# A three-part decoder layer on one core: heads-first projections, rotation by transferred halves, plain fp32 self scores

## The chip, the cores and the metric

The kernel runs on one core of a Trainium2 chip. The core has TensorE (matmuls and transposes, written PE in the rows), VectorE (DVE), ScalarE (ACT), GpSimd (POOL) and SyncE (SP), whose queue issues the transfers here. Each engine works through its own list of instructions in order and waits on semaphores. Times are microseconds (us) of one execution on the device; lower is better.

## What is computed

32 sequences of 256 tokens with 256 features go through three blocks, each added to its input and normalized. Only the first one is touched by the change: 16 query heads and 4 key and value heads of 64 features, a rotation by position, a bias linear in the distance, softmax, and the output weights. Cut to this:

```python
q = (x @ Wq).reshape(b, l, H, HD).transpose(0, 2, 1, 3)
k = (x @ Wk).reshape(b, l, KV, HD).transpose(0, 2, 1, 3)
v = (x @ Wv).reshape(b, l, KV, HD).transpose(0, 2, 1, 3)
...
q = q * cos + _rotate_half(q) * sin      # halves (x1, x2) -> (-x2, x1)
k = k * cos + _rotate_half(k) * sin
attn = jnp.einsum('bhqd,bhkd->bhqk', q, k) / math.sqrt(HD)
attn = attn + slopes[None, :, None, None] * rel[None, None, :, :]
out = jnp.einsum('bhqk,bhkd->bhqd', jax.nn.softmax(attn, axis=-1), v)
...
x = _layernorm(x + self_attention(x))
x = _layernorm(x + window_attention(x, ctx, tokens))
x = _layernorm(x + quantized_gated_ffn(x))
```

The second block is attention of windows of 64 positions to the context, the third a feed-forward part with quantized activations and three-valued weights.

## The kernel before

One batch (a sequence) is cut into named steps, and every engine has a written list of steps: `HEAD`, then `BODY` repeated with the batch number moved on by one, then `TAIL`. The repeated order runs for 27 of the 32 batches. An entry such as `(2, 'QX')` means step `QX` of the batch two behind the newest one, so three or four batches are in work at once. There is no scheduler: what stands in the list is the order of the engine, and an engine that waits holds up all that stands behind it in its list. The waits themselves are written by step kind (`at`, `freed`), so a step waits for its data and for the PSUM bank it writes, until the step that read the bank's last content has emptied it (`EMPTIED`).

The steps that the text names, in the order of the data:

- `X` splits the loaded `xT` into `x_hi` (ScalarE) and `x_lo` (GpSimd). `K`, `V` and four `Q` steps (token tile 0 or 1, column half 1 or 2) project it on TensorE by `project` (L660), each as three rounded fp32 products (high with high, low with high, high with low), tokens on partitions. ScalarE copies `Q` to `qtok` (L1353), VectorE multiplies the exchanged halves by the sines into `by_sin` (L1027), GpSimd multiplies by the cosines and adds (L1457, L1460). For `K` VectorE makes both products (L1015, L1017) and GpSimd adds (L1451).
- `kT` and `qT 0` to `qT 3` transpose the rotated tiles, so that head features lie on partitions (L644, `ktok` and `qtok`). ScalarE writes the rounded high part from PSUM, VectorE the low part (L1032, L1037).
- `S 0` to `S 7` are the self scores of two heads each (L760), again three rounded products, two heads at once on the two 64-row halves of the array. VectorE adds the distance bias and takes the row maximum (L1046), ScalarE takes the exponential (L1372), VectorE the reciprocal of the sum (`R`, L1053) and GpSimd divides (`R`, L1464).
- `T 0` to `T 15` transpose the probabilities, ScalarE copies them (L1379). `O 0` to `O 3` multiply by the values (L779), plain fp32. `W 0`, `W 1` are the output weights (L790).
- `YS`, `X1`: statistics and normalization of the sum. `NX`: its transposes; `QX`: the cross query projection, `QXT`: its transposes. `KV 0`, `KV 1`: cross keys and values from the context (L814), `KXT`: their transposes (L644, `kx_tok`), after which VectorE adds a bias (L1138) and SP fills the padded tile `kx` by eight transfers (`fill_kx`, L623). `SX 0` to `SX 3` are the cross scores, plain fp32 (L832 and L839), on banks 5 and 6; `TX`, `OX`, `BX`, `NO`, `PO` lead on to the second block's result.
- `XQ`, `G`, `U`, `HS`, `HT`, `D`, `ZS`, `out`: the third block in bf16 (L891, L901, L653, L914).

Bank 7 serves one after another `NX`, `XQ`, `QX`, `KXT`, `QXT`, `HT`, `OX`, `D`, `BX`, `NO`, `PO` and `KV`. Some fill matmuls without use (L718) stand in `HEAD` and `TAIL` only.

Of the kernel before, what the change touches and what calls it, by code (L numbers as in the profile page):

```python
# [73 lines left out]

BODY = {
    "sp": [
        (2, 'load_cell'), (3, 'load_vs'), (2, 'load_ctxT'), (3, 'fill_kx'), (2, 'load_xtok'), (2, 'load_ctx'),
        (0, 'load_xT'), (4, 'store'),
    ],
# [44 lines left out]
    "sp": [  # L124
        (0, 'first', 0), (0, 'first', 1), (0, 'first', 2), (0, 'load_xT'), (0, 'tables', 0), (0, 'loads', 0),
        (0, 'loads', 1), (0, 'load_cell'), (0, 'load_xtok'), (0, 'tables', 1), (0, 'loads', 2), (0, 'load_ctx'),
        (1, 'load_xT'), (0, 'load_ctxT'), (2, 'load_xT'), (1, 'load_ctxT'), (0, 'kx_clear'), (0, 'fill_kx'),
        (1, 'load_ctx'), (1, 'load_xtok'), (0, 'load_vs'), (1, 'load_cell'), (2, 'load_cell'), (3, 'load_xT'),
        (2, 'load_xtok'), (2, 'load_ctxT'), (1, 'load_vs'), (2, 'load_ctx'), (1, 'fill_kx'), (0, 'store'), (4, 'load_xT'),
    ],  # L130
# [1485 lines left out]
```

## Time and profile before

| what | us |
|---|---|
| median of 3 runs | 2222.89 |
| lowest and highest | 2222.48, 2224.62 |
| the profiled execution | 2226.64 |
| its span in the trace | 2224.7 |
| TensorE, VectorE, ScalarE, GpSimd busy | 2139.7, 1906.7, 1699.2, 1420.7 |

The profiled execution is 3.75 above the median, and 1.9 of it lie outside the span. A row of a timeline has the start, the length of the record, the engine, the line of the kernel, the instruction with the tile that it writes and those that it reads, and a count of instructions merged into the row; a bracket at its end is idle time ahead of it. Matmul records overlap, since the next one starts before the last one has drained: how long a step holds TensorE is read from its start to the start of the next row. A row such as `x1` where two were issued lacks a record, and the step began a little earlier.

### The profile page before, as it was taken

How to read it: one execution, taken by the hardware profiler on the slowest of the kernel's cores; microseconds unless marked ns; L12 is line 12 of the kernel's file. 1: busy time of each engine (PE TensorE's matmuls, PEld its weight loads, DVE VectorE, ACT ScalarE, POOL GpSimd, SP SyncE). 2: the span in 40 equal slices, each digit the busy share in tenths (PEclk: the TensorE clock that was granted, in tenths of full speed). 3: DMA queues.
4: the chain of work that ended last, by engine and by line, in shares of the span. 5: the costliest groups of instructions: out<-in, count | busy, mean ns of one | idle time of the engine just before them, and what ended most of it. 6: DMA issues, size and time to landing. Idle time of an engine off the chain costs nothing. (4 is left out here: it accounts for less than half of the span.)

```text
span 2224.7 us, 58431 instructions
## 1 busy us (share of the span) xinstructions
PE 2139.7 (96%) x19659; PEld 1665.7 (75%) x19722; DVE 1906.7 (86%) x7884; ACT 1699.2 (76%) x4746; POOL 1420.7 (64%) x1670
## 2 busy tenths in 40 slices
PE   7899999999999999999999999999999999999986
PEld 6677777777777777777777777777777777777764
DVE  5778888888988889988888898888988888889876
ACT  4687778887778887777888777888777788877752
POOL 2566666666766666776666676666677666667531
PEclk9999999999999999999999999999999999999999
DMA  4010101101110110110110111011011111011100
GB/s 165 11 35 25 37 25 35 27 25 37 37 36 24 28 37 26 37 37 25 35 28 25 37 37 34 26 28 37 26 37 37 25 35 28 25 37 37 27 21 11
DMA packets 85399, 74.68 MB, mean 34 GB/s; under 512 B 18544, under 2 KB 79344, under 8 KB 85104
## 3 DMA queue, kind: packets, MB, share of 16 engines
q1 hardware_dynamic: 85104, 70.93, 11.8%
q8 instruction: 163, 2.67, 0.5%
q14 instruction: 132, 1.08, 0.2%
HBM read 45.72 MB, written 8.39 MB: 24 GB/s over the span
## 5 line engine op out<-in xcount | busy, mean ns | idle before, releaser
L1464 POOL TENSOR_TENSOR prob<-prob,precs 128x512 f32<-128x512 f32 x512 | 528.5, 1040 | 551.3 <-DVE precs L1053 548.0
L1372 ACT ACTIVATE prob<-prob,nmax 128x256 f32<-128x256 f32 x1024 | 508.6, 504 | 46.0 <-DVE nmax L1046 46.0
L1046 DVE CUSTOM_DVE_ANT_0 prob<-bank,alibi 128x256 f32<-128x256 f32 x1024 | 371.5, 419 | 23.3 <-PE bank L760 23.2
L1379 ACT COPY pT<-bank 128x512 f32<-128x512 f32 x512 | 302.8, 591 | 57.0 <-PE bank L644 55.8
L644 PE MATMUL bank<-ident,prob 128*128 128x128 f32 x2048 | 316.0, 277 | 3.5 <-ACT pT L1379 3.0
L1396 ACT ACTIVATE px<-px,nmx 128x128 f32<-128x128 f32 x1024 | 313.7, 398 | 6.2 <-DVE nmx L1158 6.2
L644 PEld LDWEIGHTS bank<-ident,prob 128*128 128x128 f32 x2048 | 231.1, 141 | 55.5 <-issue 39.2
L779 PE MATMUL bank<-pT,v_sb 128*64 128x256 f32 x2048 | 250.4, 387 | 4.0 <-DVE qq_lo L1037 3.6
L1158 DVE CUSTOM_DVE_ANT_0 px<-bank,mask 128x128 f32<-128x128 f32 x1024 | 226.4, 287 | 3.7 <-issue 1.7
L779 PEld LDWEIGHTS bank<-pT,v_sb 128*64 128x64 f32 x2048 | 137.2, 137 | 101.2 <-issue 39.9
L1460 POOL TENSOR_TENSOR qtok<-qtok,by_sin 128x512 f32<-128x512 f32 x128 | 164.7, 1287 | 56.0 <-DVE by_sin L1027 46.1
L1372 ACT ACTIVATION_READ_ACCUMULATOR prob<-prob,nmax 128x1 f32 x1024 | 198.2, 194 | 0.0
L660 PE MATMUL bank<-w_hi,x_hi 128*128 128x256 f32 (+1 forms) x512 | 190.5, 372 | 4.0 <-POOL x_lo L1444 1.5
L1417 ACT ACTIVATE hh<-bank,ax 128x512 f32<-128x512 f32 x128 | 88.2, 689 | 133.2 <-PE bank L891 133.1
L1457 POOL TENSOR_TENSOR qtok<-qtok,rope 128x512 f32<-128x512 f32 x128 | 164.9, 1288 | 33.4 <-ACT qtok L1353 33.4
L660 PE MATMUL bank<-w_lo,x_hi 128*128 128x256 f32 (+1 forms) x512 | 173.2, 338 | 0.0
L660 PE MATMUL bank<-w_hi,x_lo 128*128 128x256 f32 (+1 forms) x512 | 172.8, 337 | 0.0
L760 PE MATMUL bank<-kk_hi,qq_hi 64*128 64x256 f32 x1024 | 170.6, 330 | 1.5 <-DVE kk_lo L1032 1.0
L644 PE MATMUL bank<-ident,px 128*128 128x128 f32 x1032 | 160.2, 278 | 7.3 <-ACT px L1396 2.9
L1403 ACT COPY pTx<-bank 128x512 f32<-128x512 f32 x252 | 146.5, 581 | 12.6 <-PE bank L644 12.5
L790 PE MATMUL bank<-wo_hi,oT_hi 128*128 128x256 f32 x512 | 146.2, 286 | 0.0
L760 PE MATMUL bank<-kk_hi,qq_lo 64*128 64x256 f32 x1024 | 144.2, 278 | 0.0
(223 smaller groups left out, 5950.0 us busy)
## 6 DMA issues: line engine op xcount, KB each, us to landing
raw<-in_xT SPq DMA_DIRECT2D x32, 256.0 KB, 3.0
xtok<-in_x SPq DMA_DIRECT2D x32, 256.0 KB, 2.9
kx_tok<-in_ctx SPq DMA_DIRECT2D x32, 256.0 KB, 3.0
raw<-in_ctxT SPq DMA_DIRECT2D x32, 256.0 KB, 3.0
kx<-k_sin SPq DMA_DIRECT2D x256, 32.0 KB, 2.0
vs<-vx SPq DMA_DIRECT2D x64, 128.0 KB, 2.3
out_y<-x SPq DMA_DIRECT2D x31, 256.0 KB, 3.2
cellk<-in_cell SPq DMA_DIRECT2D x32, 64.0 KB, 3.8
```

What stands on the lines that cost most here:

```text
L644: last = nc.tensor.transpose(bank[:, n * P:(n + 1) * P], src, ident[:])
L660: last = mm(to, xs[:, k, t * P:(t + 1) * P], ws[:, k, cols], start=i == 0, stop=i == KT * 3 - 1)
L760: last = mm(psum[SCORES[c]][:, q * L:(q + 1) * L], qs[half, u % 2, m, q * P:(q + 1) * P], ks[half, p // 4, :], start=i == 0, stop=i == 2)
L779: last = mm(psum[bank][c * HD:(c + 1) * HD, m * L:(m + 1) * L], v_sb[:, k, g * HD:(g + 1) * HD], pT[:, m, c, k, :], start=k == 0, stop=k = ...
L1046: v.tensor_tensor_reduce(out=prob[:, (2 * p + q) % SLOTS, c, :], in0=psum[SCORES[c]][:, q * L:(q + 1) * L], in1=alibi[:, p % 2, :], scale= ...
L1158: v.tensor_tensor_reduce(out=px[:, s % 2, i, :], in0=psum[xscores(b)[r]][:, h * P:(h + 1) * P], in1=mask[:, s % 2, :], scale=-1.0, scalar= ...
L1372: nc.scalar.activation(prob[:, (2 * p + q) % SLOTS, c, :], prob[:, (2 * p + q) % SLOTS, c, :], ACT.Exp, bias=nmax[:, i:i + 1], scale=-1.0, ...
L1379: nc.scalar.copy(pT[:, p % 2, :, :, q * P:(q + 1) * P].rearrange("p c k n -> p (c k) n"), bank[:].rearrange("p (c n) -> p c n", c=4)).then ...
L1396: ins = nc.scalar.activation(px[:, s % 2, i, :], px[:, s % 2, i, :], ACT.Exp, bias=nmx[:, 8 * s + i:8 * s + i + 1], scale=-1.0)
L1457: g.tensor_tensor(heads, heads, rope[:, 0, t:t + 1, :].to_broadcast([P, 8, HD]), ALU.mult).then_inc(sem["q_cos"], 1)
L1460: g.tensor_tensor(qtok[:, t, :], qtok[:, t, :], by_sin[:], ALU.add).then_inc(sem["rot_sum"], 1)
L1464: g.tensor_tensor(prob[:, n % SLOTS, :, :], prob[:, n % SLOTS, :, :], precs[:, 2 * n:2 * n + 2].unsqueeze(2).to_broadcast([P, 2, L]), ALU. ...
```

## The change

- `K` and the `Q` steps become five units `proj 0` to `proj 4` (unit 1 is the keys, 0, 2, 3 and 4 are the query groups 0 to 3). The weights are now the stationary operand and the tokens run through, so a unit has twelve 256-wide products, and the result has head features on partitions. `kT` and `qT` are gone.
- ScalarE writes a unit, with its scale, from the bank into `flat`. SP exchanges the halves of 32 partitions by four transfers of 64 KB into `swap`. VectorE multiplies the bank by the cosines into `turn`. GpSimd multiplies `swap` by the sines and adds `turn`, into `kk` (two buffers) or `qq` (one per group). `flat`, `swap` and `turn` have two buffers each.
- The self scores are four plain fp32 products in place of twelve rounded ones.
- The rotation table lies with features on partitions. `ZS` on GpSimd has one more wait, for `out` of the batch before. The GpSimd scratch space for transfers is made smaller.
- All step lists are written anew. Steps of the second and third block have moved too, and so have the fills in `HEAD` and `TAIL`.

```diff
+                    elif kind == "swap":
+                        n, = args
+                        i = (UNITS * b + n) % 2
+                        sp.wait_ge(*at("raw_ready", b, n))
+                        sp.wait_ge(*at("rot_sum", b, n - 2))
+                        for r in range(4):
+                            sp.dma_start(swap[r * 32:(r + 1) * 32, i, :, :], flat[(r ^ 1) * 32:(r ^ 1) * 32 + 32, i, :, :])\
+                                .then_inc(swapped[i], 16)
...
+                    elif kind == "proj":
+                        pe.wait_ge(*at("x_lo", b))
+                        pe.wait_ge(*freed(sem, bank, steps, place))
+                        parts = ((x_hi, w_hi), (x_lo, w_hi), (x_hi, w_lo))
+                        for m in range(2):
+                            first = (m if n == 1 else 4 + 2 * GROUP[n] + m) * P
+                            for i in range(KT * 3):
+                                k, (xs, ws) = i // 3, parts[i % 3]
+                                last = mm(psum[bank][:, m * L:(m + 1) * L], ws[:, k, first:first + P], xs[:, k, :], start=i == 0, stop=i == KT * 3 - 1)
...
-                        parts = ((qq_hi, kk_hi), (qq_lo, kk_hi), (qq_hi, kk_lo))
                         for q in range(2):
-                            for i, (qs, ks) in enumerate(parts):
-                                for c in range(2):
-                                    half = slice(c * HD, (c + 1) * HD)
-                                    last = mm(psum[SCORES[c]][:, q * L:(q + 1) * L], qs[half, u % 2, m, q * P:(q + 1) * P],
-                                              ks[half, p // 4, :], start=i == 0, stop=i == 2)
+                            for c in range(2):
+                                half = slice(c * HD, (c + 1) * HD)
+                                last = mm(psum[SCORES[c]][:, q * L:(q + 1) * L], qq[half, u, m, q * P:(q + 1) * P],
+                                          kk[half, b % 2, p // 4, :], start=True, stop=True)
...
+                    elif kind == "turn":
+                        dve.wait_ge(*at("raw_ready", b, n))
+                        dve.wait_ge(*at("rot_sum", b, n - 2))
+                        v.scalar_tensor_tensor(out=turn[:, i, :, :], in0=psum[home(b, "proj", n)][:].rearrange("p (m n) -> p m n", m=2),
+                                               scalar=1.0 if n == 1 else 0.125 / FACTOR[GROUP[n]],
+                                               in1=rope[:, 0:1, :].to_broadcast([P, 2, L]), op0=ALU.mult, op1=ALU.mult).then_inc(sem["rot_cos"], 1)
...
+                    elif kind == "flat":
+                        act.wait_ge(*at("proj_mm", b, n))
+                        act.wait_ge(*unit_swapped(b, n - 2))
+                        nc.scalar.activation(flat[:, i, :, :], psum[home(b, "proj", n)][:].rearrange("p (m n) -> p m n", m=2), ACT.Copy,
+                                             scale=1.0 if n == 1 else 0.125 / FACTOR[GROUP[n]]).then_inc(sem["raw_ready"], 1)
...
+                    elif kind == "turn":
+                        pool.wait_ge(*unit_swapped(b, n))
+                        g.tensor_tensor(swap[:, i, :, :], swap[:, i, :, :], rope[:, 1:2, :].to_broadcast([P, 2, L]), ALU.mult).then_inc(sem["rot_sin"], 1)
+                        pool.wait_ge(*at("rot_sin", b, n))
+                        pool.wait_ge(*at("rot_cos", b, n))
+                        pool.wait_ge(*at("S_mm", b - 1, 2 * GROUP[n] + 1 if n != 1 else -1))
+                        g.tensor_tensor(kk[:, b % 2, :, :] if n == 1 else qq[:, GROUP[n], :, :], turn[:, i, :, :], swap[:, i, :, :], ALU.add)\
+                            .then_inc(sem["rot_sum"], 1)
```

The order of VectorE in the repeated part, around the bias sum of `KXT` (the row that writes `k_sin` with 512 elements). Before, the sum stands behind `U 1` and the low part of `qT 3`, and `HS 0` follows:

```order
L1251 SCALAR_TENSOR_TENSOR hh<-hh,bank 128x512
L1255 TENSOR_TENSOR hh<-hh,bank 128x512
L1037 SCALAR_TENSOR_TENSOR qq_lo<-bank,q_scale,qq_hi 128x512
L1138 TENSOR_TENSOR k_sin<-bank,turned_bias 128x512
L1259 TENSOR_REDUCE hs<-hh 128x1
```

In the changed kernel (its own line numbers), the last of the four score instructions of `S 5` and their maximum, then `turn 1`, then the sum:

```order
L1031 ISA prob,nmax<-bank,alibi 128x256
L1031 ISA nmax 128x1
L1021 SCALAR_TENSOR_TENSOR turn<-bank,rope 128x512
L1123 TENSOR_TENSOR k_sin<-bank,turned_bias 128x512
L1236 SCALAR_TENSOR_TENSOR hh<-hh,bank 128x512
L1240 TENSOR_TENSOR hh<-hh,bank 128x512
L1244 TENSOR_REDUCE hs<-hh 128x1
```

So `S 5` has moved from behind the sum to ahead of it. The order of TensorE at the end of the feed-forward part, in bank 7. Before, with `wd` the down weights (`D 0`, `D 1`) and `hh` the transposes of `HT 1`:

```order
L914 MATMUL bank7<-wd16,hqT 128x256 x8
L644 MATMUL bank3<-ident,px 128x128 x4
L644 MATMUL bank2<-ident,prob 128x128 x4
L653 MATMUL bank7<-ident16,hh 128x128 x8
```

In the changed kernel the same two steps, with `D 1` behind them:

```order
L921 MATMUL bank7<-wd16,hqT 128x256 x8
L672 MATMUL bank7<-ident16,hh 128x128 x8
L663 MATMUL bank2<-ident,prob 128x128 x4
L663 MATMUL bank3<-ident,px 128x128 x4
L921 MATMUL bank7<-wd16,hqT 128x256 x8
```

`HT 1` now follows `D 0` with nothing between them. SP's order in the repeated part of the changed kernel, from `load_vs` on:

```order
L648 DMA vs<-vx 64x512
L649 DMA vs<-vx 64x512
L627 DMA raw<-in_ctxT 128x2x256
L621 DMA xtok<-in_x 128x2x256
L642 DMA kx<-k_sin 16x2x256 x8
L616 DMA swap<-flat 32x512 x4
L630 DMA cellq<-in_cell 128x2x1
```

Before it was

```order
L629 DMA vs<-vx 64x512
L630 DMA vs<-vx 64x512
L608 DMA raw<-in_ctxT 128x2x256
L623 DMA kx<-k_sin 16x2x256 x8
L602 DMA xtok<-in_x 128x2x256
```

so `load_xtok` has moved ahead of the fills, and a swap follows them.

## Rows read from the trace of the kernel before

**Rows 1.** The page, section 1: busy us, share of the span, instructions.

```profile
PE 2139.7 (96%) x19659; PEld 1665.7 (75%) x19722; DVE 1906.7 (86%) x7884; ACT 1699.2 (76%) x4746; POOL 1420.7 (64%) x1670
```

**Rows 2.** TensorE's timeline (start, length, engine, line, instruction, count): `V` of two batches.

```profile
1034.13 0.29 PE L660 MATMUL bank<-w_hi,x_hi 128*128 128x256 f32 x1
...
1035.58 0.60 PE L644 MATMUL bank<-ident,qtok 128*128 128x128 f32 x4
...
1099.93 0.28 PE L660 MATMUL bank<-w_hi,x_hi 128*128 128x256 f32 x1
```

**Rows 3.** TensorE's timeline: `kT`, `D 0` and the transposes behind them.

```profile
1076.93 0.60 PE L644 MATMUL bank<-ident,ktok 128*128 128x128 f32 x4
1077.67 1.03 PE L914 MATMUL bank<-wd,hqT 128*128 128x256 bf16 x8
1078.54 0.60 PE L644 MATMUL bank<-ident,px 128*128 128x128 f32 x4
1078.97 0.60 PE L644 MATMUL bank<-ident,prob 128*128 128x128 f32 x4
```

**Rows 4.** TensorE's timeline: `S 5`, `O 1`; then `SX 0` and `W 0`.

```profile
1052.77 0.39 PE L760 MATMUL bank<-kk_hi,qq_hi 64*128 64x256 f32 x2
...
1053.68 1.95 PE L779 MATMUL bank<-pT,v_sb 128*64 128x256 f32 x16
1055.56 0.65 PE L644 MATMUL bank<-ident,prob 128*128 128x128 f32 x4
...
1060.18 1.13 PE L832 MATMUL bank<-kx,qx 64*128 64x512 f32 x4
1061.24 0.39 PE L790 MATMUL bank<-wo_hi,oT_hi 128*128 128x256 f32 x1
```

**Rows 5.** TensorE's timeline: a `Q` step, a `T` step, a score step.

```profile
1057.27 0.48 PE L660 MATMUL bank<-w_hi,x_hi 128*128 128x512 f32 x1
...
1058.74 0.60 PE L644 MATMUL bank<-ident,prob 128*128 128x128 f32 x4
1059.27 0.39 PE L760 MATMUL bank<-kk_hi,qq_hi 64*128 64x256 f32 x2
```

**Rows 6.** TensorE's timeline: steps with waits; the last has it in brackets.

```profile
1040.92 0.65 PE L644 MATMUL bank<-ident,prob 128*128 128x128 f32 x4
1041.68 0.63 PE L644 MATMUL bank<-ident,xtok 128*128 128x128 f32 x4
1042.06 0.36 PE L660 MATMUL bank<-w_hi,x_hi 128*128 128x256 f32 x1
...
1043.80 0.38 PE L653 MATMUL bank<-ident,q_sin 128*128 128x128 bf16 x4
...
1068.88 1.13 PE L832 MATMUL bank<-kx,qx 64*128 64x512 f32 x4 [0.28 <-DVE nmx L1158]
```

**Rows 7.** VectorE's timeline: `qT 3`, sum of `KXT`; `S 5` and what follows it.

```profile
1051.74 0.75 DVE L1037 SCALAR_TENSOR_TENSOR qq_lo<-bank,q_scale,qq_hi 128x512 fp32r<-128x512 f32 x1
1052.40 0.68 DVE L1138 TENSOR_TENSOR k_sin<-bank,turned_bias 128x512 f32<-128x512 f32 x1
...
1056.74 0.42 DVE L1046 CUSTOM_DVE_ANT_0 prob<-bank,alibi 128x256 f32<-128x256 f32 x1
...
1058.12 0.68 DVE L1251 SCALAR_TENSOR_TENSOR hh<-hh,bank 128x512 f32<-128x512 f32 x1
```

**Rows 8.** SP's timeline of the fills; the page's DMA row (KB, us).

```profile
1053.11 5.13 SPq L623 DMA_DIRECT2D kx<-k_sin  x8
...
kx<-k_sin SPq DMA_DIRECT2D x256, 32.0 KB, 2.0
```

**Rows 9.** GpSimd's timeline: `YS` begins, `K`'s sum, `R 8` with `R 9`.

```profile
1045.06 0.23 POOL L1471 TENSOR_SCALAR y_var<-y_mv 128x2 f32<-128x2 f32 x1
...
1049.59 1.31 POOL L1451 TENSOR_TENSOR ktok<-ktok,by_sin 128x512 f32<-128x512 f32 x1
1050.85 2.05 POOL L1464 TENSOR_TENSOR prob<-prob,precs 128x512 f32<-128x512 f32 x2
```

More of the change, by code:

```diff
@@ L72 @@
 RAW = 8
+UNITS = 5
+GROUP = {0: 0, 2: 1, 3: 2, 4: 3}
 BODY = {
[L76 to L79, printed above, removed]
     "pe": [
[10 rows of a table removed]
[10 rows of a table added]
     ],
     "dve": [
[10 rows of a table removed]
[9 rows of a table added]
     ],
     "act": [
[8 rows of a table removed]
[8 rows of a table added]
     ],
     "pool": [
[4 rows of a table removed]
[5 rows of a table added]
+    ],
+    "sp": [
+        (3, 'load_vs'), (2, 'load_ctxT'), (2, 'load_xtok'), (3, 'fill_kx'), (1, 'swap', 1), (2, 'load_cell'),
+        (2, 'load_ctx'), (1, 'swap', 2), (0, 'load_xT'), (1, 'swap', 3), (1, 'swap', 4), (4, 'store'), (0, 'swap', 0),
     ],
@@ L123 @@
 HEAD = {
[L124 to L130, printed above, removed]
@@ L166 @@
     ],
     "dve": [
-        (0, 'first', 0), (0, 'first', 1), (0, 'first', 2), (0, 'prep', 0), (0, 'tables', 0), (0, 'K'), (0, 'Q', 0, 1),
-        (0, 'prep', 1), (0, 'prep', 2), (0, 'prep', 3), (0, 'Q', 1, 1), (0, 'prep', 4), (0, 'tables', 1), (0, 'qT', 0),
[30 rows of a table removed]
+        (0, 'first', 0), (0, 'first', 1), (0, 'first', 2), (0, 'prep', 0), (0, 'tables', 0), (0, 'turn', 0),
+        (0, 'turn', 1), (0, 'prep', 1), (0, 'prep', 2), (0, 'prep', 3), (0, 'prep', 4), (0, 'tables', 1),
+        (0, 'wo_split'), (0, 'turn', 2), (0, 'S', 0), (0, 'R', 0), (0, 'R', 1), (0, 'S', 1), (0, 'R', 2),
@@ L200 @@
+        (0, 'turn', 3), (0, 'prep', 6), (0, 'S', 2), (0, 'R', 3), (0, 'prep', 7), (0, 'S', 3), (0, 'turn', 4),
[27 rows of a table added]
     ],
     "act": [
-        (0, 'first', 0), (0, 'first', 1), (0, 'first', 2), (0, 'X'), (0, 'tables', 0), (0, 'Q', 0, 1), (0, 'Q', 1, 1),
[28 rows of a table removed]
+        (0, 'first', 0), (0, 'first', 1), (0, 'first', 2), (0, 'X'), (0, 'flat', 0), (0, 'tables', 0), (0, 'flat', 1),
+        (0, 'flat', 2), (0, 'prep', 4), (0, 'wo_split'), (0, 'S', 0), (0, 'S', 1), (0, 'V'), (0, 'flat', 3),
[26 rows of a table added]
     ],
     "pool": [
[15 rows of a table removed]
+        (0, 'X'), (0, 'turn', 0), (0, 'turn', 1), (0, 'R', 0), (0, 'turn', 2), (0, 'R', 1), (0, 'turn', 3),
[13 rows of a table added]
@@ new lines @@
+        (3, 'turn', 4),
+    ],
+    "sp": [
+        (0, 'first', 0), (0, 'tables', 0), (0, 'load_xT'), (0, 'first', 1), (0, 'first', 2), (0, 'loads', 0),
+        (0, 'swap', 0), (0, 'load_ctx'), (0, 'loads', 1), (0, 'load_cell'), (1, 'load_xT'), (0, 'swap', 1),
+        (0, 'tables', 1), (0, 'loads', 2), (0, 'swap', 2), (0, 'swap', 3), (0, 'swap', 4), (0, 'load_ctxT'),
+        (0, 'load_xtok'), (1, 'swap', 0), (1, 'swap', 1), (1, 'swap', 2), (1, 'swap', 3), (1, 'load_cell'),
+        (1, 'swap', 4), (2, 'load_xT'), (2, 'swap', 0), (0, 'fill_kx'), (1, 'load_ctx'), (1, 'load_ctxT'),
+        (1, 'load_xtok'), (2, 'swap', 1), (0, 'load_vs'), (2, 'swap', 2), (3, 'load_xT'), (2, 'load_cell'),
+        (2, 'swap', 3), (2, 'swap', 4), (1, 'load_vs'), (3, 'swap', 0), (2, 'load_xtok'), (2, 'load_ctxT'),
+        (3, 'swap', 1), (1, 'fill_kx'), (3, 'swap', 2), (2, 'load_ctx'), (3, 'swap', 3), (4, 'load_xT'), (0, 'store'),
+        (3, 'swap', 4), (4, 'swap', 0),
@@ L251 @@
 TAIL = {
[L252 to L256 removed]
[22 rows of a table removed]
[19 rows of a table added]
+        (31, 'fill', 3, 8), (31, 'G', 3), (31, 'HT', 0), (31, 'fill', 5, 4), (31, 'fill', 3, 16), (31, 'fill', 5, 4),
+        (31, 'D', 0), (31, 'HT', 1), (31, 'D', 1), (31, 'fill', 3, 8),
     ],
     "dve": [
[18 rows of a table removed]
[16 rows of a table added]
     ],
     "act": [
[13 rows of a table removed]
[13 rows of a table added]
     ],
     "pool": [
[7 rows of a table removed]
[8 rows of a table added]
+    ],
+    "sp": [
+        (29, 'load_vs'), (30, 'load_xtok'), (30, 'load_ctxT'), (30, 'load_cell'), (29, 'fill_kx'), (30, 'load_ctx'),
+        (31, 'swap', 1), (31, 'swap', 2), (31, 'swap', 3), (31, 'load_ctxT'), (31, 'swap', 4), (28, 'store'),
+        (31, 'load_cell'), (30, 'load_vs'), (31, 'load_xtok'), (30, 'fill_kx'), (31, 'load_ctx'), (29, 'store'),
+        (31, 'fill_kx'), (31, 'load_vs'), (30, 'store'), (31, 'store'),
     ],
@@ L337 @@
 EMPTIED["prep", 5] = ("w_mean", 0)
-EMPTIED.update({("qT", u): ("q_ready", u) for u in range(4)})
+EMPTIED.update({("proj", n): ("rot_cos", n) for n in range(UNITS)})
 EMPTIED.update({("O", u): ("oT_ready", u) for u in range(4)})
@@ L417, in at, with unit_swapped @@
             return (sem[name], count) if count > 0 else (sem["begun"], 1)
+        swapped = [ctx.enter_context(nc.semaphore(f"swapped{i}")) for i in range(2)]
+        def unit_swapped(batch, n):
+            unit = UNITS * batch + n
+            return (swapped[unit % 2], 64 * (unit // 2 + 1)) if unit >= 0 else (sem["begun"], 1)
         def landed(name, batch):
@@ L464, in build @@
         v_sb = sb("v_sb", [P, TT, KV * HD])
-        by_sin = sb("by_sin", [P, 512])
-        ktok = sb("ktok", [P, TT, KV * HD])
-        qtok = sb("qtok", [P, TT, 8 * HD])
-        kk_hi = sb("kk_hi", [P, 2, L], F32R)
-        kk_lo = sb("kk_lo", [P, 2, L], F32R)
-        qq_hi = sb("qq_hi", [P, 2, 2, L], F32R)
-        qq_lo = sb("qq_lo", [P, 2, 2, L], F32R)
+        flat = sb("flat", [P, 2, 2, L])
+        swap = sb("swap", [P, 2, 2, L])
+        turn = sb("turn", [P, 2, 2, L])
+        kk = sb("kk", [P, 2, 2, L])
+        qq = sb("qq", [P, 4, 2, L])
         prob = sb("prob", [P, SLOTS, 2, L])
@@ L730, in run @@
                         last.then_inc(sem["V_mm"], 1)
-                    elif kind == "Q":
-                        t, c = args
-                        pe.wait_ge(*freed(sem, bank, steps, place))
-                        pe.wait_ge(*at("x_lo", b))
-                        project(2, t, psum[bank][:], slice(512 * c, 512 * c + 512)).then_inc(sem["proj_mm"], 1)
-                    elif kind == "kT":
-                        pe.wait_ge(*at("rot_sum", b, 0))
-                        pe.wait_ge(*freed(sem, bank, steps, place))
-                        transposes(psum[bank], [ktok[:, t, h * P:(h + 1) * P] for h in range(2) for t in range(TT)])\
-                            .then_inc(sem["kT_mm"], 1)
-                    elif kind == "qT":
-                        u, = args
-                        pe.wait_ge(*at("rot_sum", b, 2 if u < 2 else 4))
-                        pe.wait_ge(*freed(sem, bank, steps, place))
-                        transposes(psum[bank], [qtok[:, t, (2 * (u % 2) + m) * P:(2 * (u % 2) + m + 1) * P]
-                                                for m in range(2) for t in range(TT)]).then_inc(sem["qT_mm"], 1)
                     elif kind == "S":
@@ L1572, in constants @@
     cos, sin = rope_table(L, HD, 0)
-    rope = np.concatenate([by_tile(cos), by_tile(sin * np.where(np.arange(HD) < HD // 2, -1.0, 1.0))], axis=1)
+    turned = np.stack([cos, sin * np.where(np.arange(HD) < HD // 2, -1.0, 1.0)]).transpose(0, 2, 1)
+    rope = np.concatenate([turned, 2.0 * turned], axis=1).transpose(1, 0, 2).reshape(P, 2 * L)
     rel = (np.arange(L)[None, :] - np.arange(P)[:, None]).astype(np.float32)
     alibi = np.stack([np.float32(2.0 ** (-0.5 - m / 2)) * rel for m in range(2)], axis=1).reshape(P, -1)
-    q_scale = np.array([[0.125 / FACTOR[u] * 4.0 ** (p // HD) for u in range(4)] for p in range(P)])
     ropex = []
@@ L1586, in constants @@
     second = k > WIN + q % WIN
-    return dict(rope=f(rope), alibi=f(alibi), q_scale=f(q_scale), ropex=f(np.concatenate(ropex, axis=1)), pen=f(np.concatenate([first, second], axis=1)))
+    return dict(rope=f(rope), alibi=f(alibi), ropex=f(np.concatenate(ropex, axis=1)), pen=f(np.concatenate([first, second], axis=1)))
 def kernel(**inputs):
```

96 lines of the change are left out of this document (21 added, 75 removed), and 382 rows, old and new, of tables (BODY, HEAD, TAIL).

## The prediction

> **What bounds the kernel now.** I read the page's busy shares first, then TensorE's timeline over one batch, then what each engine waits for in that stretch. TensorE is busy for 96% of the span, VectorE for 86%, ScalarE for 76%, GpSimd for 64% [rows 1]. A busy share alone doesn't prove a bound, because a matmul's record is longer than the slot it takes: the reader should go by the distance from one start to the next. The value projection of one batch starts at 1034.13 and that of the next at 1099.93, so a batch takes 65.80 us [rows 2]. Walking through that batch, step start to step start, almost every step begins where the one before leaves off. The visible waits are few: 0.31 behind the key transposes [rows 3], and in [rows 6] 0.31 before the transposes of `NX` (0.76 where 0.45 is usual), 0.29 between `K` and `XQ` (1.74 where 1.45 is usual) and 0.28 before a cross score step. They sum to 1.19 us. So about 64.6 of the 65.8 us are matmul slots, and the kernel is bound by TensorE's slots. Work taken from the other engines counts only where TensorE waits for it.
>
> **Transposes removed.** Four `qT` steps and `kT` go, each four fp32 transposes. Neighbouring transposes of that shape stand 0.43 apart, and the step after a product in another form takes a little more [rows 3]; I take 0.44. Five of them in 32 batches: 5 x 0.44 x 32 = 70 us off. They lie on TensorE itself, so all of it counts.
>
> **Projections.** Before, a `Q` step of six 512-wide products takes 1.47, and there are four; `K` has twelve 256-wide ones, like `V`, whose twelve take 1.45 [rows 2, 5]. After, there are five units of twelve 256-wide products. 4 x 1.47 + 1.45 = 7.33 becomes 5 x 1.45 = 7.25, with the same number of columns. The doubled number of weight loads doesn't show in `V`. I add 0.1 per batch for five entries into the step from other forms: +3 us; the ends are -3 and +6.
>
> **Self scores.** Before, a step has twelve 64-row products, two at a time on the two halves of the array: 0.91 us [rows 4]. After, there are four plain fp32 products. Two rows bound their cost. The values product `O` has eight plain fp32 products of 256 columns (recorded as 16) in 1.88, so four of them would be 0.94. The first cross score step has two plain fp32 products of 512 columns on the same two 64-row halves, which is as many columns as the new step has: 1.06 [rows 4]. I take 1.03, near the second, since only it uses the 64-row halves. 8 x 32 x 0.12 = +31 us; the ends +0.03 and +0.15 give +8 and +38.
>
> **Other engines.** VectorE loses per batch two 0.68 products of `K`, four of `Q`, `kT` and four `qT`, about 7.8 us of records, and gains five `turn` products like the 0.75 of the old `qT` [rows 7]: some 4 us less. ScalarE loses nine copies and gains five. GpSimd goes from nine adds and products of 1.26 to ten [rows 9]. None is the bound, so I price these at nothing directly; they shift the waits. VectorE's relief is why I expect the 0.31 before `NX` to go: that bank is freed by the last `KV` products, which stand behind `qT` now. `kT` no longer stands in front of `D`; a `T` step now lies between the projection and `XQ`; and `W` is moved behind the cross scores for which TensorE waited 0.28. So 1.19 goes, in the 27 batches of the repeated order: -32 us.
>
> **The swap.** Each unit has four transfers of 64 KB on SP. An issue takes SP 0.64 (eight in 5.13), and one lands 2.0 after its issue [rows 8]. A unit is swapped some 1.9 + 2.0 + 0.6 = 4.5 us after it is flattened, and the least distance I find in the new order between a flattened unit and GpSimd's `turn` is about 10 us of TensorE time (`flat 3` to `turn 3`). They are hidden. Behind `swap` in SP's queue stand `load_cell`, `load_ctx` and `load_xT`, all due most of a batch later. In front of `fill_kx`, the one tight transfer, there is now `load_xtok`, which waits for `X1`; that is done before `KXT`'s sum.
>
> **New waits of the order.** Two places look worse. First, `KXT` to `SX 0`. On VectorE the sum of `KXT` was directly behind the last `qT`; it now stands behind a whole self score step and a `turn`. From the start of the transposes: 0.3 until the last score product has ended (a record's length, [rows 2]), 1.38 for the score step (1056.74 to 1058.12), 0.66 for `turn`, 0.68 for the sum [rows 7] make 3.0; the eight fills then need 4.5 to the last issue (seven eighths of 5.13) and 2.0 to land [rows 8], with 0.1 for semaphores: 9.6. TensorE reaches `SX 0` after four transpose steps of 0.44, five bf16 steps (two `G`, two `U`, `HT 0`) of 0.43, since `D 0`'s eight bf16 products of 256 columns take 0.87 [rows 3] and these have half the columns, `O` 1.88, a projection 1.45, a score step 1.03 and four changes of form of 0.1 (a `T` step before a score step takes 0.53 [rows 5] in place of 0.43), together 8.7. So it waits 0.9. Second, `HT 1` now follows `D 0` directly in the same bank 7, which a 256-wide sum of VectorE must empty (0.45, taken as two thirds of the 0.68 of a 512-wide one [rows 7]); before, two steps lay between. With the tail of the matmul and two semaphores I take 0.7. 27 x 1.6 = +43 us. Ends: nothing, if VectorE runs ahead, and 2.5.
>
> **Head and tail.** The first batch waits for tables, weights and their preparation, and the fills that were spread over its waits are put elsewhere; the last batch's chain doesn't hold the changed steps. I take 0, with 5 either way.
>
> **Sum.** -70 + 3 + 31 - 32 + 43 = -25 us. The profiled execution took 2226.6 around a span of 2224.7, 3.7 above the median of 2222.9; the change of 25 applies to either, and on the median gives 2198.
>
> **One rule against the change.** The row of [rows 4] says that plain fp32 on the two halves takes 1.06 where three rounded products take 0.91. The Trainium skill, "FP8 and Floating Point Precision", section "TensorE Precision Notes", states that true fp32 makes four passes through the array (high and low parts each with each), where the sum of three products makes three. By that rule alone the step would be 4/3 as long.
>
> **The rivals.**
> 1. *Full price of the scores, slower.* If the new step costs 4/3 of the old, 0.91 x 4/3 = 1.21, then scores alone cost 0.30 x 256 = +77 instead of +31, and the sum is 2198 + 46 = 2244. From +0.22 a step the kernel is no faster. Against it: the 1.06 of [rows 4] is measured for plain fp32 on the same halves with the same number of columns. For it: the row's step has only half as many weight loads. (The factor 4/3 is that of the Trainium skill's page named above.)
> 2. *GpSimd's queue becomes late, slower.* Between `R 6` and `R 8` it now has R 1.0, `turn 4` 2.5, R 1.0, `YS` with `X1` 4.5, the key sum 1.26, the query sum 1.26, R 1.0, so 12.6 us [rows 9], while TensorE goes from `NX` to `T 8` in some 13.6. The slack is 1.0; before, even `R 9` was done at 1052.90 [rows 9] and `T 8` began at 1055.56 [rows 4], a slack of 2.7 and more. With two operations more of lateness, 2.5, TensorE waits 1.5 to 2 us a batch: 27 x 1.8 = +49, 2247. It decides from 1.0 + 0.9 us of lateness.
> 3. *The two new waits don't come.* If VectorE or the fills run ahead: 2198 - 43 = 2155.
> 4. *The halves don't overlap in plain fp32.* Then a step costs near 1.06 + 0.85: +0.88 x 256 = +225, 2400. The 1.06 speaks clearly against it.
> 5. *A wash.* Half of the waits of rival 2: about 2222.
>
> **How the numbers follow.** Forecast 0.55 (2180 to 2215), rival 3 0.18, rival 1 0.06, rival 2 0.11, rival 4 0.02, rival 5 0.08. A measurement of this kernel tells apart about 0.2%, 4.4 us. Faster 0.73, same 0.08, slower 0.19. The range 2145 to 2245 takes in rival 3 with the low end for the scores, and rivals 1, 2 in part; about 2 in 10 lie outside.
>
> **What would show it.** The batch distance on TensorE should be 65.0 (65.8 now); a score step 1.03; a projection unit 1.45 to 1.5; `SX 0` should wait for the fills and `HT 1` for the sum of `D 0`; swaps should have landed before `turn` starts. If GpSimd's `turn` waits for a swap, or `T` steps wait for GpSimd, rival 2 is right and I am wrong.

## The result and the profile after

The changed kernel takes 2272.75 us (median of 4 runs, 2270.81 to 2273.45), the kernel before 2223.48 beside it (4 runs, 2222.48 to 2224.62). The ratio is 1.022, 95% interval 1.0202 to 1.0238. It is 49 us slower where 25 us faster was forecast, and it lies outside the range. The profiled execution took 2273.45 around a span of 2271.6.

The page of the changed kernel, section 1, answers to [rows 1]. TensorE is busy as long as before, with 833 matmul records less (the program issues 60 matmuls less in a batch, but a plain fp32 product is recorded twice). VectorE has 59 us less, not the 4 x 32 = 128 that the prediction took from it.

```profile
PE 2137.0 (94%) x18826; PEld 1631.3 (72%) x18826; DVE 1847.4 (81%) x7692; ACT 1647.0 (73%) x4618; POOL 1459.4 (64%) x1702
```

TensorE's timeline over one batch of the repeated order, from one `KXT` to the next (start, length, engine, line, instruction, count, and in brackets the idle time ahead of it): `HT 0`, `SX 0`, `D 0`, `HT 1`.

```profile
1009.03 0.66 PE L663 MATMUL bank<-ident,kx_tok 128*128 128x128 f32 x4
...
1017.17 0.62 PE L672 MATMUL bank<-ident,hh 128*128 128x128 bf16 x8
1018.66 1.13 PE L839 MATMUL bank<-kx,qx 64*128 64x512 f32 x4 [0.87 <-issue]
...
1036.07 1.04 PE L921 MATMUL bank<-wd,hqT 128*128 128x256 bf16 x8
1038.42 0.61 PE L672 MATMUL bank<-ident,hh 128*128 128x128 bf16 x8 [1.31 <-DVE x L1265]
...
1075.66 0.66 PE L663 MATMUL bank<-ident,kx_tok 128*128 128x128 f32 x4
```

The batch takes 1075.66 - 1009.03 = 66.63, where it was 65.8 [rows 2] and 65.0 was forecast. `HT 0` holds TensorE 0.55 when the next step is ready (`a_kxt`, below), so `SX 0` waited 1.49 - 0.55 = 0.94. The prediction had 0.9, and its parts come out too: 9.63 from `KXT` to `SX 0` (9.6 predicted), 8.69 of it TensorE's own path (8.7). `D 0` runs 0.87 [rows 3], so `HT 1` waited 2.35 - 0.87 = 1.48, twice the 0.7 of the prediction. Without both waits a batch is 64.2 long.

**Why `HT 1` waited 1.5.** VectorE's timeline ahead of the sum of `D 0` (the row that writes `x`), and GpSimd's at the same time:

```profile
1034.45 0.58 DVE L1127 CAST cellqf<-cellq 128x2 f32<-128x2 int32 x1
1035.07 2.48 DVE L1130 SCALAR_TENSOR_TENSOR mask<-cellk,cellqf,pen 128x128 f32<-128x128 int32 x2
1037.58 0.29 DVE L1133 TENSOR_SCALAR mask<-mask 128x256 f32<-128x256 f32 x1
1037.79 0.48 DVE L1265 SCALAR_TENSOR_TENSOR x<-bank,hs,x 128x256 f32<-128x256 f32 x1
```

```profile
1033.73 1.28 POOL L1431 TENSOR_TENSOR swap<-swap,rope 128x512 f32<-128x512 f32 x1
1035.08 1.27 POOL L1435 TENSOR_TENSOR qq<-turn,swap 128x512 f32<-128x512 f32 x1
1036.31 1.09 POOL L1440 TENSOR_TENSOR prob<-prob,precs 128x512 f32<-128x512 f32 x1
```

`D 0` had ended by 1037.1, and its sum began at 1037.79, since VectorE's `mask` stood in front of it. In the kernel before, `mask` stands in front of the sum of `D 1`. And `mask` had become long: its two products took 2.48 together, as long as the two GpSimd instructions beside them (1035.08 to 1037.40). The groups of the whole execution say that this is the rule: first the kernel before, then the changed one (busy us, then mean ns).

```profile
L1145 DVE SCALAR_TENSOR_TENSOR mask<-cellk,cellqf,pen 128x128 f32<-128x128 int32 x64 | 19.7, 349 | 1.1
L1142 DVE CAST cellqf<-cellq 128x2 f32<-128x2 int32 x32 | 5.2, 163 | 0.0
```

```profile
L1130 DVE SCALAR_TENSOR_TENSOR mask<-cellk,cellqf,pen 128x128 f32<-128x128 int32 x64 | 70.7, 1143 | 1.1
L1127 DVE CAST cellqf<-cellq 128x2 f32<-128x2 int32 x32 | 17.2, 537 | 0.0
```

The same instruction takes 1143 ns in place of 349, and the small cast 537 in place of 163: together 63 us of VectorE's time, of the 128 - 59 = 69 by which its relief fell short. In a step order where `mask` runs with no GpSimd instruction beside it, it takes 361 again (`a_mask`, below). With its old lengths the step would have been done by 1034.45 + 0.16 + 0.70 + 0.29 = 1035.6, before `D 0` ended, so by this estimate it is the length and not the place alone that made the wait. The Trainium skill, "SBUF — State Buffer", section "Who interferes with whom", states that a VectorE instruction with two inputs in SBUF contends with a GpSimd instruction that reads SBUF, that the pair of ports they share is an exclusive lock, and that issue order decides who blocks. The trace agrees: the two products last as long as the two GpSimd instructions beside them (2.48 us for both, against 1.27 and 1.09).

**The irregular batches.** Not every batch takes 66.6. Of 26 distances between `KXT` steps (335.0 to 2088.8), 13 are 66.61 to 66.65; six, each fourth one, are 69.38 to 69.82; the others lie between. The sum above 66.62 is 21.6 us, 0.8 a batch: 12.4 of it are longer waits of `SX 0`, and the rest is 1.5 in each of the six long batches, behind the wait. One of the long ones, on SP (the fills, then the swap), and on TensorE (`HT 0`, `SX 0`, first instructions of `W 0`):

```profile
1145.89 5.18 SPq L642 DMA_DIRECT2D kx<-k_sin  x8
1151.17 3.21 SPq L616 DMA_DIRECT2D swap<-flat  x4
```

```profile
1151.06 0.62 PE L672 MATMUL bank<-ident,hh 128*128 128x128 bf16 x8
1153.86 1.50 PE L839 MATMUL bank<-kx,qx 64*128 64x512 f32 x4 [2.17 <-issue]
1155.29 0.58 PE L797 MATMUL bank<-wo_hi,oT_hi 128*128 128x256 f32 x1
1155.66 0.41 PE L797 MATMUL bank<-wo_hi,oT_lo 128*128 128x256 f32 x1
1155.88 0.41 PE L797 MATMUL bank<-wo_lo,oT_hi 128*128 128x256 f32 x1
```

The fills were issued on time, but `SX 0` began 2.79 after the end of the last issue, in a usual batch 1.48. In three other batches the eight issues themselves took 5.8 in place of 5.18.

The trace says what stands beside the late landings. Of the 27 groups of fills from 338 us on, up to the one at 2092, seven landed 2.5 to 3.0 after the last issue. In each of these seven a packet of 16 KB on the instruction queue q8 started 0.38 to 0.52 after the last issue and took 1.0 to 1.5; the fills landed 1.0 to 1.2 after that packet's end. In none of the other 20 does such a packet start between the last issue and the landing, and they landed 1.4 to 1.6 after it. In the kernel before, from 330 us on to 2050, no such packet starts in the first 1.1 us behind a last issue, and the fills landed within 1.5, but for one group at 1.87. It is a coincidence in time and not a proof: no run took the instruction loads away.

Behind the long waits the clock fell: the windows (us, busy of PE, PEld, DVE, ACT, POOL, granted clock, DMA share, GB/s) show it.

```profile
1151.00:1154.00 3.00, 0.83 (x12) 0.62 (x12) 1.97 (x10) 2.08 (x8) 2.79 (x3) 1.00 0.31 68
1154.00:1155.00 1.00, 1.00 (x4) 0.16 (x4) 0.00 (x0) 0.00 (x0) 0.09 (x1) 0.74 0.32 76
1155.00:1156.00 1.00, 1.00 (x5) 0.71 (x4) 0.47 (x5) 0.13 (x1) 0.00 (x0) 0.50 0.33 66
```

0.50 is the lower of the two levels, 1.2 GHz: the products of `W 0` stand 0.21 apart in place of 0.12. The six long batches, in which `SX 0` waited 2.16 to 2.59, have such a stretch of 3.4 us each; that is their 1.5. One with a wait of 2.03 and all with shorter ones have none. In the kernel before, no such stretch lies between 100 and 2100 us; there `SX 0` did not wait.

### The profile page after: what moved, and what is told of

It reads as the page before. It is cut to its first block and busy times, and to the rows that moved or that the text cites. A ratio compares the mean times of both kernels' runs of the same rounds, so it can differ in the third digit from the quotient of the medians.

```text
span 2271.6 us, 57273 instructions
## 1 busy us (share of the span) xinstructions
PE 2137.0 (94%) x18826; PEld 1631.3 (72%) x18826; DVE 1847.4 (81%) x7692; ACT 1647.0 (73%) x4618; POOL 1459.4 (64%) x1702
## 5 line engine op out<-in xcount | busy, mean ns | idle before, releaser
L767 PE MATMUL bank<-kk,qq 64*128 64x256 f32 x2048 | 292.3, 404 | 0.0
L1431 POOL TENSOR_TENSOR swap<-swap,rope 128x512 f32<-128x512 f32 x160 | 205.3, 1283 | 28.3 <-DMA swap<-flat 21.8
L767 PEld LDWEIGHTS bank<-kk,qq 64*128 64x128 f32 x2048 | 177.2, 187 | 59.8 <-issue 41.7
L748 PE MATMUL bank<-x_hi,w_hi 128*128 128x256 f32 x640 | 196.2, 307 | 3.1 <-DVE turn L1021 2.5
L748 PE MATMUL bank<-x_lo,w_hi 128*128 128x256 f32 x640 | 180.2, 282 | 0.0
L748 PE MATMUL bank<-x_hi,w_lo 128*128 128x256 f32 x640 | 179.9, 281 | 0.0
L663 PEld LDWEIGHTS bank<-ident,px 128*128 128x128 f32 x1032 | 114.0, 141 | 80.9 <-issue 48.4
L1435 POOL TENSOR_TENSOR qq<-turn,swap 128x512 f32<-128x512 f32 x128 | 162.7, 1271 | 10.0
```

What stands on the lines that cost most here:

```text
L663: last = nc.tensor.transpose(bank[:, n * P:(n + 1) * P], src, ident[:])
L748: last = mm(psum[bank][:, m * L:(m + 1) * L], ws[:, k, first:first + P], xs[:, k, :], start=i == 0, stop=i == KT * 3 - 1)
L767: last = mm(psum[SCORES[c]][:, q * L:(q + 1) * L], qq[half, u, m, q * P:(q + 1) * P], kk[half, b % 2, p // 4, :], start=True, stop=True)
L1431: g.tensor_tensor(swap[:, i, :, :], swap[:, i, :, :], rope[:, 1:2, :].to_broadcast([P, 2, L]), ALU.mult).then_inc(sem["rot_sin"], 1)
L1435: g.tensor_tensor(kk[:, b % 2, :, :] if n == 1 else qq[:, GROUP[n], :, :], turn[:, i, :, :], swap[:, i, :, :], ALU.add)\
```

## The experiments

Times are medians, ratios are to the kernel before beside it. All edits are of the repeated order alone, unless said otherwise.

### The waits by themselves

`a_kxt`: `KXT` and VectorE's sum of it ahead of `S 5`.

```diff
 pe
-    (3, 'U', 1), (1, 'T', 7), (1, 'S', 5), (2, 'KXT'), (3, 'U', 2)
+    (3, 'U', 1), (2, 'KXT'), (1, 'T', 7), (1, 'S', 5), (3, 'U', 2)
 dve
-    (3, 'U', 1), (1, 'S', 5), (0, 'turn', 1), (2, 'KXT')
+    (3, 'U', 1), (2, 'KXT'), (1, 'S', 5), (0, 'turn', 1)
```

> The changed kernel with the KXT transposes and VectorE's sum of them each moved ahead of score step S 5, in the repeated order alone. Theory A (the loss is made of two waits of TensorE for work that VectorE has late: SX 0 1.6 us, HT 1 1.4 us a batch): the wait before SX 0 goes, 27 x 1.6 = 43 us off, 2230; and if the half clock of every fourth batch follows the waits, 7 x 2.9 = 20 more, 2210. Rival B (the half clock belongs to the new matmul forms, whatever the waits): 2230 and still one half-clock stretch in four batches. Rival C (something else on VectorE or SP is late next, so that the wait only moves): 2260 or more.

2233.38 us, ratio 1.0039 (1.0024 to 1.0054): 39 us of the 49 are gone. A batch takes 65.95. The half clock between 100 and 2100 us is gone, so is the wait of `SX 0`; 0.27 of it came back ahead of `KXT`. Theory A's mechanism holds, with its clock part, but not its size: it had 63 us off, from a wait of 1.6. The wait is 0.94 in a usual batch and 1.4 in the mean, and each half clock cost 1.5 and not 2.9. In sum, the fills' chain cost 66.63 - 65.95 = 0.7 in a usual batch and all of the irregular 0.8.

`a_dose`: the same sum moved only past `turn 1`.

```diff
 dve
-    (1, 'S', 5), (0, 'turn', 1), (2, 'KXT')
+    (1, 'S', 5), (2, 'KXT'), (0, 'turn', 1)
```

> The changed kernel with only one thing moved: VectorE's sum of KXT from behind turn 1 to ahead of it (0.66 earlier), in the repeated order. Theory A: the wait before SX 0 falls from 1.6 to about 0.95, 27 x 0.66 = 18 us off, 2255, and the half clock of every fourth batch stays or goes with the wait (2235 to 2255). Rival B (SX 0 waits for something else than this sum): 2272.

2241.71 us, ratio 1.0077 (1.0062 to 1.0092). The wait in a usual batch fell from 0.94 to 0.35, by the 0.6 that the sum came earlier, and the longest one from 338 us on is 1.3; between 230 and 2170 us the clock is full. So one instruction of 0.6 us, moved, gave 31 us: 0.6 x 27 = 16 directly, 9 since the six half clocks are gone, and 6 since the transfers came late by less. No fill of the repeated order landed more than 1.6 after the last issue here; where a 16 KB packet of q8 stood in that gap, it started 1.03 or later.

`b_wait`: the opposite, in the kernel before.

```diff
 dve
-    (2, 'KXT'), (3, 'HS', 0)
+    (3, 'HS', 0), (2, 'KXT')
```

> The kernel before with VectorE's sum of KXT behind HS 0 (a reduction and four small steps, about 1.8 us), in the repeated order: a wait before SX 0 in an order and with matmul forms that have no half clock. If the half clock comes from such a wait and not from the changed matmul forms: the wait costs 27 x 0.5 to 1.5 = 13 to 40 us and stretches at half clock appear in the steady part, each 3 us more, up to 60 in all. If it comes from the forms: the same 13 to 40 us, and the clock stays full.

2265.28 us, ratio 1.0175 (1.0158 to 1.0192). `SX 0` waits 1.35 in a usual batch (36 us in 27), and three batches, those with waits of 2.4, 2.7 and 3.3, have half clock behind them (one with 2.2 has not). This is read from the profiled execution, which took 2276.02, the longest of the four. The half clock comes from the wait, with either kernel's matmuls.

`a_ht`: `mask` behind `D 1`, and two steps between `D 0` and `HT 1`. `a_both`: this with `a_kxt`.

```diff
 pe
-    (3, 'D', 0), (3, 'HT', 1), (1, 'T', 14), (2, 'TX', 3, 0), (3, 'D', 1), (1, 'T', 15)
+    (3, 'D', 0), (1, 'T', 14), (2, 'TX', 3, 0), (3, 'HT', 1), (1, 'T', 15), (3, 'D', 1)
 dve
-    (1, 'mask'), (3, 'D', 0), ..., (3, 'D', 1), (0, 'S', 1)
+    (3, 'D', 0), ..., (3, 'D', 1), (1, 'mask'), (0, 'S', 1)
```

> The changed kernel with VectorE's mask step moved from ahead of the sum of D 0 to behind that of D 1, and with one T and one TX step between D 0 and HT 1 on TensorE, in the repeated order alone. Theory A: the wait before HT 1 goes, 27 x 1.4 = 38 us off, 2235, and 2215 if the half clock follows the waits. Rival B: 2235 with the half clock left as it is. Rival C: the wait moves to another place behind it, such as D 1 or the next score step, 2260 or more.

> Both edits together. Theory A: both waits go, 81 us off, 2192; without the half clock 2172, and a batch takes 63.7 on TensorE, which is faster than both kernels. Rival B: 2192 with a half-clock stretch in every fourth batch. Rival C: the sum of the two gains is under 50 us, 2225 or more, because one wait hides behind the other.

`a_ht` 2272.87 us, ratio 1.0212 (1.0197 to 1.0228), nothing gained; `a_both` 2231.80, ratio 1.0031 (1.0018 to 1.0043), as `a_kxt`. Both are rival C. The wait of `HT 1` is gone and two others stand in its place; TensorE's timeline of `a_both`, then ScalarE's:

```profile
1088.80 0.66 PE L663 MATMUL bank<-ident,px 128*128 128x128 f32 x4 [0.54 <-ACT px L1375]
1089.29 0.61 PE L672 MATMUL bank<-ident,hh 128*128 128x128 bf16 x8
1090.53 0.63 PE L663 MATMUL bank<-ident,prob 128*128 128x128 f32 x4 [0.63 <-ACT pT L1358]
```

```profile
1087.46 2.45 ACT L1375 ACTIVATE px<-px,nmx 128x128 f32<-128x128 f32 x8
1089.81 0.57 ACT L1358 COPY pT<-bank 128x512 f32<-128x512 f32 x1
```

The exponential of the cross scores began at 1087.46 and is a third done at 1088.26, when `TX 3` wants its first half, and the copy of `T 14` stands behind it, which `T 15` waits for. ScalarE has no idle time there for 12 us. In that order TensorE came too early with `TX 3`.

`a_mask`: `a_kxt` and `mask` behind `D 1`, TensorE's order of `D 0`, `HT 1`, `T 14` left.

```diff
 dve
-    (1, 'mask'), (3, 'D', 0), ..., (3, 'D', 1), (0, 'S', 1)
+    (3, 'D', 0), ..., (3, 'D', 1), (1, 'mask'), (0, 'S', 1)
```

> The changed kernel with KXT moved on TensorE and VectorE as in a_kxt, and VectorE's mask step behind the sum of D 1 as in a_both, but with TensorE's order D 0, HT 1, T 14, TX 3, D 1, T 15 left as the change has it. In a_both the wait went from HT 1 to two places that ScalarE releases: TX 3 (0.6, the exponential of the cross scores) and T 15 (0.8, the copy of T 14, which stands behind that exponential in ScalarE's list). Theory A2 (ScalarE's list is late there, and the steps between D 0 and T 15 should stand so that its lateness is covered): only the 0.7 of HT 1 behind D 0 is left, a batch takes 65.1 to 65.3, 2208 to 2215, faster than both kernels. Rival (the ring of S 0, its exponential and T is itself the bound, whatever the order): 65.9 a batch as in a_both, 2230.

2216.56 us, ratio 0.9963 (0.9950 to 0.9976), faster than both kernels. A batch takes 65.30. `mask` takes 361 ns now, with no GpSimd instruction beside it in the repeated order:

```profile
L1130 DVE SCALAR_TENSOR_TENSOR mask<-cellk,cellqf,pen 128x128 f32<-128x128 int32 x64 | 20.5, 361 | 1.1
```

```profile
1016.90 1.04 PE L921 MATMUL bank<-wd,hqT 128*128 128x256 bf16 x8
1018.61 0.61 PE L672 MATMUL bank<-ident,hh 128*128 128x128 bf16 x8 [0.67 <-DVE x L1265]
```

The wait of `HT 1` is 1.71 - 0.87 = 0.84, near the 0.7 of the prediction. Against `a_kxt`, moving `mask` alone gives 17 us.

`a_t7`: `a_mask` with `KXT` behind `T 7` on TensorE.

```diff
 pe
-    (2, 'KXT'), (1, 'T', 7), (1, 'S', 5)
+    (1, 'T', 7), (2, 'KXT'), (1, 'S', 5)
```

> The kernel of a_mask with KXT on TensorE behind T 7 in place of ahead of it, in the repeated order. In a_mask 0.27 is left before KXT, for the sum of QX that empties bank 7; T 7 covers it, less 0.07 for one change of form. 27 x 0.2 = 5 us off, 2211. Rival (it only moves to SX 0 or to ScalarE's list, as in a_best): 2216.

2207.40 us, ratio 0.9928 (0.9916 to 0.9940), the fastest of those that do the whole work: a batch takes 65.0. `a_best`: besides, `TX 2` (second half) between `D 0` and `HT 1`, and ScalarE's copy of it behind the exponential of `SX 3`.

```diff
 pe
-    (2, 'TX', 2, 1), (3, 'D', 0), (3, 'HT', 1)
+    (3, 'D', 0), (2, 'TX', 2, 1), (3, 'HT', 1)
 act
-    (2, 'TX', 2, 1), (2, 'SX', 3)
+    (2, 'SX', 3), (2, 'TX', 2, 1)
```

> The kernel of a_mask with three more moves in the repeated order: TX 2 (second half) from ahead of D 0 to between D 0 and HT 1 on TensorE; on ScalarE the exponential of SX 3 ahead of the copy of that TX; KXT on TensorE behind T 7 in place of ahead of it. In a_mask 0.84 is left before HT 1 and 0.27 before KXT. Theory A2 (these waits lie in the order alone): both go but for 0.1 to 0.3, a batch takes 64.3 to 64.6, 2216 less 27 x 0.8 = 2194 to 2200. Rival (ScalarE's list is the bound there): the wait moves to TX 3 or T 15, 2216 or more.

2217.50 us, ratio 0.9964 (0.9952 to 0.9977), 10 us worse than without these two moves. TensorE's timeline of `a_best`:

```profile
1018.56 0.61 PE L672 MATMUL bank<-ident,hh 128*128 128x128 bf16 x8 [0.23 <-DVE x L1265]
1019.00 0.61 PE L663 MATMUL bank<-ident,prob 128*128 128x128 f32 x4
1020.14 0.63 PE L663 MATMUL bank<-ident,px 128*128 128x128 f32 x4 [0.54 <-ACT pTx L1382]
```

`TX 3` writes the bank that this copy empties, and the copy now stood behind 2.45 us of exponentials. The wait moved again.

### What TensorE's slots are worth

`b_s32`: the kernel before with plain fp32 scores of the high parts.

```diff
-                        parts = ((qq_hi, kk_hi), (qq_lo, kk_hi), (qq_hi, kk_lo))
...
+                                last = mm(psum[SCORES[c]][:, q * L:(q + 1) * L], qq_hi[half, u % 2, m, q * P:(q + 1) * P].bitcast(F32),
+                                          kk_hi[half, p // 4, :].bitcast(F32), start=True, stop=True)
```

> The kernel before, with four plain fp32 products of the high parts in place of the twelve rounded ones of a self score step; the products with the low parts are left out. The price of the scores alone. Theory A: a step takes 1.06 in place of 0.91, 256 x 0.15 = 38 us more, 2261. Rival of the prediction (four passes in place of three, 1.21): 77 more, 2300. Rival B (plain fp32 forms bring the half clock): 2261 plus some 20 us, and stretches at 0.5 of the clock that the kernel before doesn't have.

2250.06 us, ratio 1.0111 (1.0096 to 1.0126): 25 us more, 0.10 a step, below both theories. A step takes 1.07 where it took 0.91, and part of it fell on waits that were there. The ratio is 1.18 and not the 4/3 (1.21 a step) that rival 1 takes from the four passes of the Trainium skill, "FP8 and Floating Point Precision", section "TensorE Precision Notes". The forms bring no half clock.

`b_quarter`: the kernel before with one transpose of four in `kT` and `qT`; the other three are left out, so its output is not the block's.

```diff
-                                                for m in range(2) for t in range(TT)]).then_inc(sem["qT_mm"], 1)
+                                                for m in range(2) for t in range(TT)][:4 if b < 2 else 1]).then_inc(sem["qT_mm"], 1)
```

> The kernel before with one transpose in place of four in every kT and qT step from the third batch on (the other three quarters of the bank keep old values; all else runs as before). What TensorE's slots alone are worth. The prediction's step (every slot counts): 30 x 5 x 0.44 x 0.75 = 50 us off, 2174. Rival D (the other engines are so near that freed slots become waits): less than 25 us off, 2200 or more, with new waits on TensorE released by ScalarE or VectorE. In between: each of the two in part.

2221.37 us, ratio 0.9984 (0.9975 to 0.9993): 3 us off, not 50. The four `qT` steps took 0.58 a batch in place of 1.86, and TensorE waited instead. Its waits over four batches (920 to 1190 us; total, times, longest), first before, then `b_quarter`:

```profile
PE bank L832 <- DVE nmx L1158: 1.2, 4, 0.4
PE bank L891 <- issue: 0.6, 4, 0.2
```

```profile
PE bank L832 <- DVE nmx L1158: 2.4, 4, 0.6
PE bank L914 <- ACT ox L1408: 1.8, 4, 0.5
PE bank L832 <- DVE qx L1107: 1.3, 2, 0.8
PE bank L644 <- DVE vx L1133: 0.8, 4, 0.2
PE bank L644 <- ACT pTx L1403: 0.8, 4, 0.2
```

7.1 us in place of 1.8, 1.3 a batch more, as much as was freed in `qT`. `b_light`: besides, VectorE and ScalarE work only on 64 of 512 columns in these steps (one of the four operations shown).

```diff
-                        nc.scalar.copy(kk_hi[:], bank[:].rearrange("p (h n) -> p h n", h=2)).then_inc(sem["k_hi"], 1)
+                        nc.scalar.copy(kk_hi[:, :, :(256 if b < 2 else 32)], bank[:].rearrange("p (h n) -> p h n", h=2)[:, :, :(256 if b < 2 else 32)]).then_inc(sem["k_hi"], 1)
```

> The kernel of b_quarter, and besides the five kT and qT operations of VectorE and of ScalarE in a batch work from the third batch on only on 64 of 512 columns (the rest keeps old values). It tells why 50 us of freed slots gave 3. Theory E (VectorE and ScalarE stand so near behind TensorE that slots are worth something only when their work goes too): VectorE has 5 x 0.5 and ScalarE 5 x 0.4 less a batch, and the freed slots now count, 2180 to 2190. Rival F (waits that lie in the written order and the length of the chain through the engines, not in their load): 2210 or more.

2192.01 us, ratio 0.9860 (0.9844 to 0.9876): 29 us off `b_quarter`. It is near theory E (2180 to 2190) and far from rival F. Slots and the other engines' work together gave 32 us where the slots alone gave 3. How much the lighter work would give with all transposes left in, no run shows.

`a_slots`: `a_mask` with four idle transposes ahead of each projection unit.

```diff
+                        transposes(psum[bank], [ident[:]] * 4)
                         parts = ((x_hi, w_hi), (x_lo, w_hi), (x_hi, w_lo))
```

> The kernel of a_mask with four more fp32 transposes (of the identity, into the bank that the unit then overwrites) ahead of each projection unit, 20 a batch: about the slots that kT and qT took, given back with no work for another engine. Theory S (in the new order, where VectorE has less to do, TensorE's slots do count in full): 32 x 5 x 0.44 = 70 us more, 2287. Rival D (as in b_quarter, where 50 us of freed slots gave 3: the rings through the other engines set the batch, and slots lie in slack): less than 20 us more, 2235 or less.

2274.38 us, ratio 1.0220 (1.0204 to 1.0236): 58 us more than `a_mask`. Such a step of four holds TensorE 0.37, where 0.44 was expected, so 160 steps make 59. Theory S: in this order, slots count in full.

## Why the prediction was wrong, step by step

Per usual batch of the repeated order:

| | predicted | measured |
|---|---|---|
| batch without the two waits | 63.4 | 64.2 |
| wait of `SX 0` | 0.9 | 0.94 |
| wait of `HT 1` | 0.7 | 1.48 |
| late transfers and half clock, mean | 0 | 0.8 |
| sum | 65.0 | 67.4 |

Three terms of some 21 us each in 27 batches make 64 of the 75 us between forecast and result. The forecast also took the terms of the matmuls over all 32 batches, where the five outer ones have their own order; what that is worth was not measured. Head and tail, taken as 0, stayed near it: the 26 distances grew by 44 us together, the span by 47.

- **Transposes.** They went, and in an order where VectorE has less to do, slots counted (`a_slots`, and `b_light` in part). But the reason given was wrong: "bound by TensorE's slots" was read from waits of 1.2 a batch, and `b_quarter` shows that in the kernel before freed slots turned into waits at once. A short list of waits says that TensorE is the bound now, not by how much.
- **Projections.** Mis-sized: a unit takes 1.50 to 1.52 with its changes of form, and one of 1.61 behind a bf16 step, where 1.45 and 0.02 were taken: 0.2 to 0.3 a batch.
- **Scores.** 1.06 to 1.07 a step (1.03 predicted), some 9 us too little in all. In the kernel before the new form costs 25 us (`b_s32`), since part of it falls on waits. Rivals 1 and 4 are out, and the time that the prediction gives rival 4 was added up wrongly: 2198 + 225 is 2423, not 2400.
- **Changes of form, the missing term.** Where transposes had stood beside transposes (0.43 apart), the ones that remain now stand oftener beside another form. In the changed kernel, the timeline of `SX 1` and what follows:

```profile
1023.66 1.09 PE L846 MATMUL bank<-kx,qx 64*64 64x512 f32 x8
1024.68 0.66 PE L663 MATMUL bank<-ident,px 128*128 128x128 f32 x4
1025.18 0.60 PE L663 MATMUL bank<-ident,prob 128*128 128x128 f32 x4
1025.71 1.14 PE L767 MATMUL bank<-kk,qq 64*128 64x256 f32 x8
```

  A `TX` step behind a score step holds TensorE 0.50, a `T` step ahead of one 0.53. The eight `TX` steps sum to 4.25 a batch, 3.88 before. It was charged to the projections and in part to the path to `SX 0`, never to the removed steps' neighbours.
- **Old waits.** Those of `NX`, `kT` and `XQ` went; of the 0.28 before a cross score step 0.13 is left, before `SX 2`. Right but for that.
- **`SX 0`.** The chain (the sum, the fills' issue to 8.15 behind `KXT`, the landing) and the 0.94 are as predicted. The term failed in its tail: the wait makes TensorE hang on a transfer, and every fourth landing is late by 1.1 to 1.7, after which the clock halves. The term put this at nothing. No row of the kernel before could have shown it, for there the fills of the repeated order landed on time.
- **`HT 1`.** The place was right, and without `mask` its wait is 0.84. What was missed is that the change also moved `mask` from ahead of the sum of `D 1` to ahead of the sum of `D 0`, beside a busy GpSimd.
- **Other engines, "price these at nothing directly".** Wrong for VectorE: 63 us of its relief were lost beside GpSimd, and that gave `HT 1` its longer wait.
- **GpSimd's queue and the swap.** From the fifth batch to the last but one every swap landed at least 4.5 us before its `turn`, and TensorE waited for none; rival 2 is out. GpSimd did wait for swaps in the first three batches and once in the last, 21.8 us in all, which the prediction's "they are hidden" leaves out.

Open: whether the instruction load beside each late landing is its cause; the loads were not taken away in any run. Also open is what of `a_t7`'s head and tail could still be had; only the repeated order was changed.

## What to carry to other kernels

Before counting freed slots as gain, ask what each next engine in the ring has left; a run that frees slots and nothing else tells it. Where a step list is written anew, list for every critical wait not only the step that answers it but all that stands ahead of it on the answering engine, and what the neighbour engine does at that time. Never let TensorE be the first to miss a transfer: a wait of 0.9 that looks cheap carries the transfer's late landings and the clock with it.
